# Moving the x-branch convolution ahead of the output projection in a fused state-space and mixture-of-experts layer

## What is computed

```python
xz = einsum('bld,ed->ble', layernorm(x), in_proj_w)      # 1024 -> 2048
x, z = split(swapaxes(xz, 1, 2), 2)                      # x half, z half
x = silu(dwconv_same(x, conv_x_w))                       # 4 taps
z = silu(dwconv_same(z, conv_z_w))
x_dbl = einsum('bdl,ed->ble', x, x_proj_w)               # 64 + 16 + 16
dtr, Bm, Cm = split(x_dbl)
delta = softplus(dt_proj(dtr) + dt_proj_b)
h = exp(delta * A) * h + (delta * x) * B ;  y = (h * C).sum(n) + D * x   # per token
s = einsum('bld,ed->ble', concat([y, z]), out_proj_w)
g = silu(top-2-of-8 gated experts(xn) + shared expert(xn))
out = x_in + s * g
```

## Time and profile before

| | |
|---|---|
| time, median of 2 runs | 4530.35 us (4524.61 and 4536.1) |
| the profiled execution | 4463.0 us, span of its slowest core (core 6) 4461.5 us |
| spans of the 8 cores | 4405.3 to 4461.5 us |
| TensorE (PE) busy | 58% of the span |
| VectorE (DVE) busy | 51% |
| ScalarE (ACT) busy | 45% |
| GpSimd (POOL) busy | 6% |

### The profile page before, as it was taken

One profiled execution on the slowest core, in us unless ns is written; L12 is line 12 of the kernel. 1 busy time (PEld: TensorE's weight loads), 2 busy tenths in 40 slices (PEclk: granted clock), 3 DMA queues, 4 the chain that ended last, 5 costly groups with the idle time before them and its releaser, 6 DMA issues.

```text
span 4461.5 us, 70363 instructions; the slowest of 8 cores (4405.3 to 4461.5 us)
## 1 busy us (share of the span) xinstructions
PE 2595.6 (58%) x17792; PEld 1938.1 (43%) x17792; DVE 2275.5 (51%) x2949; ACT 2028.2 (45%) x4233; POOL 267.4 (6%) x386
## 2 busy tenths in 40 slices
PE   2104766675656657456565756656575665657566
PEld 1103544454444535344454534444353454435344
DVE  0205364464745456474545648454564845456484
ACT  1204363453635445463644546363454636354463
POOL 0100010100101010000101000010100001010000
PEclk9557767676687878777777877877787787778777
DMA  7796333343443434343433434433343433334343
GB/s 117 117 112 145 122 125 110 115 147 94 135 122 128 129 114 147 109 128 122 129 119 121 140 109 128 128 124 119 132 129 109 128 128 125 117 133 128 110 132 104
DMA packets 329923, 549.76 MB, mean 123 GB/s; under 512 B 20457, under 2 KB 170090, under 8 KB 324530
## 3 DMA queue, kind: packets, MB, share of 16 engines
q1 hardware_dynamic: 319554, 473.49, 33.8%
q0 software_dynamic: 9968, 71.77, 8.4%
HBM read 557.31 MB, written 46.47 MB: 135 GB/s over the span
## 4 chain that ended last, share of the span: by engine, by line
PE 35%; ACT 22%; DMA 17%; issue 13%; DVE 6%; another core or an unknown queue 5%; POOL 2%; SPq 0%; DVEq 0%; ACTq 0%; POOLq 0%
PE P L259 33%; ACT dA L817 8%; DMA sb_out<-blob_out 6%; DMA sb_w<-blob_w 3%; ACT scrb L933 3%; ACT L933 2%; DMA x_f<-x_t 2%; DMA sb_cd<-blob_cd 2%; POOL delta L697 1%; DMA sb_in<-blob_in 1%; PE P L526 1%; DMA bc_dram<-bcB 1%; ACT stage L680 1%; DVE g_f L508 1%
## 5 line engine op out<-in xcount | busy, mean ns | idle before, releaser
L846 DVE TENSOR_TENSOR_SCAN h_b<-dA,carry,dBx 128x1024 bf16<-128x1024 f32 x480 | 1128.4, 2351 | 82.7 <-DVE dA L842 82.3
L817 ACT ACTIVATE dA<-delta,A_neg 128x256 f32<-128x256 f32 x2048 | 858.6, 496 | 622.2 <-DVE fixt L829 590.4
L259 PE MATMUL P<-xn_b,sb_w 128*128 128x256 bf16 x4096 | 649.7, 328 | 559.0 <-ACT scrb L933 428.7
L259 PEld LDWEIGHTS P<-xn_b,sb_w 128*128 128x128 bf16 x4096 | 460.7, 116 | 743.5 <-issue 617.4
L259 PE MATMUL P<-scrb,sb_w 128*128 128x256 bf16 x4096 | 502.9, 283 | 48.7 <-DMA sb_w<-blob_w 48.0
L259 PEld LDWEIGHTS P<-scrb,sb_w 128*128 128x128 bf16 x4096 | 412.4, 101 | 121.0 <-issue 60.4
L259 PE MATMUL P<-xn_b,sb_in 128*128 128x256 bf16 (+1 forms) x2176 | 316.5, 312 | 196.7 <-DMA sb_in<-blob_in 126.4
L810 DVE TENSOR_TENSOR dBx<-u_b,Bb 128x4096 bf16<-128x4096 bf16 x128 | 294.1, 2298 | 245.6 <-DMA Bb<-bc_dram 179.1
L933 ACT ACTIVATE scrb<-P,b1c 128x256 bf16<-128x256 f32 x512 | 242.4, 473 | 316.0 <-PE P L259 279.1
L943 DVE TENSOR_TENSOR scrb<-scrb,ge_all 128x1024 bf16<-128x1024 bf16 x128 | 88.5, 691 | 545.2 <-PE P L259 287.6
L259 PE MATMUL P<-xzh,sb_cd 128*128 128x256 bf16 x1024 | 188.1, 355 | 303.0 <-DMA sb_cd<-blob_cd 155.6
(11 more groups left out here) (115 smaller groups left out, 2517.8 us busy)
## 6 DMA issues: line engine op xcount, KB each, us to landing
sb_w<-blob_w SPq DMA_DIRECT2D x512, 512.0 KB, 4.3
sb_in<-blob_in SPq DMA_DIRECT2D x256, 256.0 KB, 3.4
sb_out<-blob_out SPq DMA_DIRECT2D x128, 512.0 KB, 4.4
sb_cd<-blob_cd SPq DMA_DIRECT2D x128, 256.0 KB, 3.7
Bb<-bc_dram POOLq DMA_DIRECT2D x16, 1024.0 KB, 5.1
Cb<-bc_dram POOLq DMA_DIRECT2D x16, 1024.0 KB, 7.0
blob_w<-w_w POOLq DMA_DIRECT2D x2, 8192.0 KB, 115.4
out<-stage SPq DMA_DIRECT2D x32, 512.0 KB, 3.2
```

Of the source, the lines that this page charges most:

```text
L259: return eng.matmul(out_ap, lhsT, rhs, start=first, stop=last, skip_group_check=True)
L817: return eng.activation(sb["dA"][:, slot * 256:(slot + 1) * 256], sb["delta"][:, g * 256:(g + 1) * 256], AF.Exp, scale=sb["A_neg"][:, g * ...
L846: return eng.tensor_tensor_scan(sb["h_b"][:, q0 * 256:(q0 + 4) * 256], apv(sb["dA"], s0 * 256, [[1, 1024]]), apv(sb["dBx"], dko + q0 * 256 ...
```

## The change

The call of `conv_phase(i, 0)` moves from behind `out_proj_phase_a(i-1)` and `out_proj_a_evac(i-1)` to ahead of them. No function changes.

```diff
             if i >= 1:
                 scan_group(i - 1, GSPLIT + 1)
+            if i < NCH:
+                conv_phase(i, 0)
+            if i >= 1:
                 out_proj_phase_a(i - 1)
                 out_proj_a_evac(i - 1, (6, 7, 4, 5, 0, 1, 2, 3))
-            if i < NCH:
-                conv_phase(i, 0)
             if i >= 1:
                 idents_phase(i - 1, GSPLIT, first=True)
```

## The result

The changed kernel takes 4595.42 us (median of 11 runs, 4573.62 to 4650.59); the kernel before, now with 10 runs, 4472.96 us. The changed one is slower by the ratio 1.0302, 95% interval 1.0278 to 1.0325. The forecast was a factor of 1.031. The time in microseconds, 4670, was 1.6% too high, because the two runs known before (4530) lay 1.3% above the median of ten; scaled from the profiled execution, as 4601, it would have been right to 0.1%. In some executions of every kernel the cores of one die have a lower granted clock and the time is longer: every ratio is taken from the executions without this (the two medians alone stand 1.0274 apart), and in the profiles in which it shows only cores 0 to 3 are compared, with cores 0 to 3.

The account below looks back on a forecast made before the run. A chain that changes engines bounds the kernel. Per boundary 7.15 - 0.56 + 0.4 + 1.0 + 1.2 = 9.2 us, times 15 is 138 us on 4463.0, factor 1.031; scaled to the runs' median, 4670 us, range 4590 to 4725.

Parts of the forecast that it names:

- The chain: At each chunk boundary, the start of the sums over the states sets the time: a microsecond there is one of the chunk.
- third rival: DVE's 13.98 us wait at the boundary's end absorbs the delay, so it costs nothing: 4530 us; chance 0.04.
- The convolution's input: Ahead of the convolution PE waits uncovered for ACT's `xzh` evictions: +7.15 us a boundary, less 0.56 for the wait that goes.
- The output projection's first loads: First `sb_out` load, behind convolution load 3 on SP, lands 7.4 us after the convolution's start, nearly covered: +0.4 us a boundary.
- The sums' bank: The sums wait for ACT to evict output projection from P7, now between the two stages: +1.0 us a boundary.
- The clock: After 7 us without work the convolution's first two taps run at PE's lower clock: +1.2 us a boundary.
- The second rival: PE's clock falls and stays, a slow piece behind each load wait: 12.8 us a boundary, 4655 or 4725 us; chance 0.14.
- The first rival: Output projection runs free of its load waits in its new place: -0.7 us a boundary, 4520 us; chance 0.06.
- scaled to it, 4530.35 x 1.031: Factor 1.031 applied to the median of the runs shown, 1.5% above the profiled execution: 4670 us.

Follow-up runs that it names:

- Run 5: The move made at only 7 of the 15 boundaries (i = 1 to 7), the rest ordered as in the kernel before; ratio to the kernel before 1.0109.
- run 1: Changed kernel with the small DVE halo copy into `xzh` moved ahead of scan group 6; ratio to the kernel before 1.0158.
- run 2: Control: the kernel before, with the small DVE halo copy into `xzh` moved ahead of scan group 6; ratio to the kernel before 1.0009.
- Run 3: Changed kernel with `sb_out` loads 0 and 1 issued ahead of all the convolution's loads; ratio to the kernel before 1.0277.
- run 6: Changed kernel with the second half of the output projection's last 16 matmuls writing bank P7 first; ratio to the kernel before 1.0256.
- run 4: Changed kernel with 56 added matmuls, their result unread, filling PE's wait ahead of the convolution; ratio to the kernel before 1.0301.
- run 10: run 9 with `sb_out` loads 4 and 5 issued behind `sb_cd` loads 2 and 3; ratio to the kernel before 0.9843.
- run 7: Convolution put between the output projection's y and zc parts, `sb_out` loads 4, 5 and first two `sb_cd` loads issued early; ratio to the kernel before 0.9914.
- run 9: Convolution's taps 0, 1 between y part and `sb_out` load 4, taps 2, 3 between loads 5 and 6, P7 first; 0.9687 of the kernel before, 4319.33 us.
- run 8: run 7 with `sb_out` loads 4 and 5 issued behind `sb_cd` loads 2 and 3; ratio to the kernel before 0.9862.

## Why the prediction was right

The forecast had the cause, the largest term and the factor right. Its agreement to 0.001 is in part luck: the wait was 0.6 us a boundary larger than forecast, and the 0.5 us that the sums give back, which it did not have, cancel most of that.

*The chain.* That the start of the sums over the states is the number to follow held: they start 9.8 us later and the chunk's period is 9.3 us longer. Run 5 shows that the price is per boundary. The slack of DVE (third rival) moved with the x projection: DVE still waits for B, 12.85 us in the sixth boundary against 13.98 in the earlier trace rows.

```profile
1938.86 2.31 DVE L810 TENSOR_TENSOR dBx<-u_b,Bb 128x4096 bf16<-128x4096 bf16 x1 [12.85 <-DMA Bb<-bc_dram]
```

*The convolution's input.* The largest term, 7.15 - 0.56 = 6.6, measured 7.24; it was worked out from three boundaries of one core. Runs 1 and 2 show its cause from both sides.

*The output projection's first loads.* 0.4 expected, 0.23 as the gap. At the sixth boundary the first `sb_out` load landed about 9.3 us after the convolution's start (4.0 to its issue at 1887.94, 5.3 for the load) and not 7.4, mostly because the first taps ran at the lower clock; the convolution had become longer by the same cause and covered most of it. Run 3 confirms the gap.

*The sums' bank.* +1.0, measured +1.09; run 6 takes it away.

*The clock.* +1.2 expected for both stages, 0.88 + 0.36 measured, and run 4 shows 0.7 of the convolution's 0.9 to be clock. The output projection's 0.36 is not shown to be: it did not change when the clock ahead of it did, and run 2 differs from the kernel before by as much. The first taps did begin at 1.2 GHz in all 120 boundaries. The rule of the Trainium skill (TensorE: Matmul & The Clock Gate, section "HAM oscillation — how this bites in real kernels"), that bursts between waits for DMAs begin slow, holds for the wait of 7 us, and in run 10 for one of 6.7. The prediction said that the trace does not agree with it for the output projection, and this was a misreading: 0.93 is a mean over 23 us, and the row behind the wait of 3.75 us has 32 matmuls in 5.32 us where the `y_b` row has 32 in 3.65. The trace agrees behind that wait, in both kernels (0.56 before and 0.54 after). Behind the projection's shorter waits it agrees less: 0.87 behind 2.0 us and 0.96 behind 1.5 us in the kernel before, as means. The second rival did not come, since what it would add behind the longest wait was being paid before the change too, and the projection's mean stayed at 0.84 (0.86 before).

*The first rival* (the output projection's load waits vanish in the new place) did not come either: 25.2 us. Runs 7 and 9 show what it would have taken: other work in those waits, since with two slots only two loads can be early.

*Where it was off.* In the base, above all. The step "scaled to it, 4530.35 x 1.031" took the median of two runs as the kernel's time; ten runs gave 4473, near the profiled execution. The range, 4590 to 4725, hung on the same base for most of its width, so the measured 4595 lies at its low end. Not foreseen, and small, was the 0.5 us a boundary given back by the sums' own matmuls, which run at a higher clock in their new place.

## What to carry to other kernels

A stage moved forward on an engine that runs in order costs the wait for its input that the displaced stage used to cover. So ask for each stage when its input is there and what covers the time until then; both can be read from the timeline, from more than one boundary. The same list of waits tells the better place: cut up a stage whose input is there and put its pieces where the engine waits for loads (here 3% gained, where the move as a whole lost 3%). Then check the order of the loads on the issuing queue, which decides which of two waits is the short one. Read the clock per piece of matmuls and not as the mean of a stage.

## What the runs showed of the hardware

- With two loads of 256 KB issued just ahead of it, a load of 512 KB took 5.10 us to land in place of 4.07, on top of an issue 2.5 us later (run 10 against run 9); with two loads of 512 KB ahead of it, one of 256 KB took 4.67 us in place of 2.93 (run 7 against run 8).
- A long wait of PE is paid for again in the clock of what follows. Behind 7.87 us, 16 matmuls took about 3.5 us (changed kernel), behind 5.45 us 3.49 (run 10), behind 3.74 us 3.30 (kernel before), behind 2.17 us 2.32 (run 9), where 1.91 is the length at the upper clock; all are means over 120 boundaries.
- The length of the wait alone does not tell the clock behind it. In run 1, behind a wait of 2.46 us on the mean, the convolution's first 8 matmuls ran at 0.67; in the kernel before, behind a wait of 2.02 us, the third piece of the output projection ran at 0.87. What makes the difference is not shown.
- With 56 matmuls put into the wait of 7.9 us the first 8 taps ran at 0.96 and the next 8 at 0.87, where the changed kernel had 0.50 and just above. The last 8, behind their own waits for loads, stayed at 0.61, so the convolution had 0.80 on the mean (run 4, cores 0 to 3).
